# Window attention with the score and value matmuls of two sequences issued together, one ring of seven PSUM banks, and the row maximum subtracted on GpSimd

## What is computed

```python
x = x + 0.5 * ffn_ref(layernorm(x), ...)      # "stack" 0: 6 layers
x = x + attn_ref(layernorm(x), ...)           # a gated state-space scan, 16 states
x = x + 0.5 * ffn_ref(layernorm(x), ...)      # "stack" 1: the same 6 layers again
# one layer of ffn_ref (16 heads of 64, windows of 32):
q, k, v = split(shift_tokens(x) @ Wqkv)
q, k = rotary(l2norm(q) * qs), rotary(l2norm(k) * ks)
sim = where(mask, -max, einsum('bhwie,bhwje->bhwij', q, k_of_this_and_last_window) * 8)
x = softmax(sim) @ v_of_this_and_last_window @ Wo + x
a, gate = split(layernorm(shift_tokens(x)) @ W1 + b1)
x = (a * gelu(gate)) @ W2 + b2 + x
```

## Time and profile before

| | |
|---|---|
| median of 3 runs | 3716.87 us (3713.0 to 3719.67) |
| profiled execution, its own time | 3724.61 us |
| span of its instructions | 3722.6 us |
| stack 0, scan, stack 1, by the slices | about 1690, 350 and 1690 us |

### The profile page before, as it was taken

How to read it: one execution, slowest core, us unless ns; L and a number is a source line. 1 busy time by engine, 2 the same in 40 slices (tenths; PEclk the granted TensorE clock), 3 DMA queues, 4 the chain that set the end, 5 groups by cost and what they waited for, 6 DMA issues and landing times.

```text
span 3722.6 us, 144192 instructions
## 1 busy us (share of the span) xinstructions
PE 3402.5 (91%) x62248; PEld 1871.9 (50%) x62248; DVE 3223.6 (87%) x5344; ACT 2227.8 (60%) x3808; POOL 2052.1 (55%) x1787
## 2 busy tenths in 40 slices
PE   6899999999999999985676799999999999999996
PEld 2455555555555555542333355555555555555553
DVE  5899999999999999874776799999999999999984
ACT  3566576665666666652453466666766667666663
POOL 3666566555666656642433565665656656565552
PEclk8999999999999999996877999999999999999998
DMA  4232332232332322200001332232232332332320
GB/s 126 68 79 70 75 81 73 72 81 70 80 77 70 85 70 72 73 17 12 0 0 54 78 76 73 70 87 69 73 85 67 78 83 67 77 82 66 77 49 24
DMA packets 200483, 250.08 MB, mean 67 GB/s; under 512 B 52012, under 2 KB 95656, under 8 KB 199848
## 3 DMA queue, kind: packets, MB, share of 16 engines
q1 hardware_dynamic: 199848, 240.86, 25.9%
HBM read 36.18 MB, written 3.15 MB: 11 GB/s over the span
## 4 chain that ended last, share of the span: by engine, by line
PE 30%; DVE 12%; issue 4%; ACT 3%; POOL 1%; DMA 1%; SPq 0%; POOLq 0%; DVEq 0%; ACTq 0%
PE general L566 4%; PE attp L580 4%; PE general L628 3%; PE scores L598 3%; PE sums L608 2%; PE general L636 2%; PE general L645 2%; PE general L638 1%; PE proj_k L554 1%; DVE k_ring L1232 1%; DVE sines L752 1%; DVE q_ring L758 1%; DVE probs_t L845 1%; PE proj_q L554 1%; PE proj_q L556 1%
## 5 line engine op out<-in xcount | busy, mean ns | idle before, releaser
L1107 POOL TENSOR_TENSOR k_ring<-k_ring,partner 128x512 f32<-128x512 f32 x384 | 499.0, 1299 | 362.1 <-DMA partner<-sines 359.9
L1116 POOL TENSOR_TENSOR probs<-probs,q_scale 128x512 f32<-128x512 f32 x384 | 401.8, 1046 | 396.8 <-DVE probs L828 396.8
L1122 POOL TENSOR_TENSOR probs<-probs,row_sum 128x512 f32<-128x512 f32 x384 | 407.8, 1062 | 358.3 <-DVE row_sum L839 358.2
L1107 POOL TENSOR_TENSOR q_ring<-q_ring,partner 128x512 f32<-128x512 f32 x384 | 491.2, 1279 | 50.4 <-DMA partner<-sines 50.4
L954 ACT ACTIVATE squares<-proj_q 128x512 f32<-128x512 f32 x384 | 229.0, 596 | 402.4 <-PE proj_q L556 401.0
L580 PEld LDWEIGHTS attp<-probs_t,v_buf 32*64 32x64 f32 x24576 | 393.0, 133 | 147.4 <-issue 141.8
L566 PE MATMUL general<-att,wo 128*128 128x512 f32 x768 | 376.2, 624 | 74.0 <-ACT att L1013 74.0
L580 PE MATMUL attp<-probs_t,v_buf 32*64 32x64 f32 (+1 forms) x24576 | 435.5, 218 | 5.1 <-ACT att L1013 5.1
L752 DVE SCALAR_TENSOR_TENSOR sines<-proj_q,vec,consts 128x512 f32<-128x512 f32 x384 | 278.7, 726 | 170.1 <-ACT squares L954 149.7
L628 PE MATMUL general<-wv,xs 128*32 128x256 f32 x6144 | 413.2, 387 | 3.1 <-DVE rstd L727 1.7
L598 PE MATMUL scores<-k_ring,q_ring 64*32 64x64 f32 (+1 forms) x24576 | 405.0, 215 | 0.0
(11 more groups left out here) (149 smaller groups left out, 6835.5 us busy)
## 6 DMA issues: line engine op xcount, KB each, us to landing
partner<-sines SPq DMA_DIRECT2D x3072, 64.0 KB
wqk_raw<-in_wqkv SPq DMA_DIRECT2D x80, 128.0 KB
wv<-in_wqkv SPq DMA_DIRECT2D x12, 512.0 KB, 4.4
wo<-in_wo SPq DMA_DIRECT2D x12, 512.0 KB, 4.7
w<-in_w SPq DMA_DIRECT2D x12, 341.0 KB, 3.3
base_dram<-x SPq DMA_DIRECT2D x8, 256.0 KB, 2.7
att<-in_wqkv SPq DMA_DIRECT2D x4, 512.0 KB, 5.8
q_ring<-base_dram SPq DMA_DIRECT2D x8, 256.0 KB, 3.1
```

The lines of the kernel that those rows point to most:

```text
L1107: e.tensor_tensor(y, y, partner[:, which, :], ALU.add).then_inc(S[f"rotated_{side}"], 1)
L1116: e.tensor_tensor(y, y, spread_keys(scale), ALU.mult).then_inc(S["q_norms_off"], 1)
L1122: e.tensor_tensor(y, y, spread_keys(row_sum[:, b, :]), ALU.mult).then_inc(S["probs_done"], 1)
```

## The change

- `pe_scores` and `pe_values` take a group of four heads of **both** sequences at once, every second step. For each window they issue the four matmuls of sequence 0 and the four of sequence 1, and for sequence 1 the heads are swapped in pairs (`h = q ^ seq`), so that the eight matmuls name eight different tiles of the array (scores: 64 by 32; values: 32 by 64). Scores go to one bank per sequence, values to four.
- All banks but `sums` form one ring of seven. Each use takes the next bank and waits for the release of the use seven before.
- The row maximum is subtracted on GpSimd (`pool_sub`), one step after the scores; exp, sum and the later stages move one step back. The softmax works on 1024 columns per operation, with two buffers `probs` instead of three. Scores are still two operations.
- The copy of the key norms goes from VectorE to ScalarE (`act_k_inv`); the spread is four matmuls of 256 columns.
- The three gate matmuls and the three gelus stand in one step (p = 1), the value matmuls and products in the next two.
- The order inside a step changes on every engine; `q_scale8` is written by eight activations instead of four; the raw weight loads have three semaphores instead of one; a constant is twice as wide.

```diff
-EXP_LAG = SCORES_LAG + 1
-TURN_LAG = SCORES_LAG + 2
-VALUES_LAG = SCORES_LAG + 3
+OFF_LAG = SCORES_LAG + 1
+EXP_LAG = SCORES_LAG + 2
+TURN_LAG = SCORES_LAG + 3
+VALUES_LAG = SCORES_LAG + 4
-PROBS = 3
+PROBS = 2
...
-        self.hidden = next(((self.item(t, 25 + j), j) for j in range(len(HIDDEN_CUTS)) if self.item(t, 25 + j) is not None), None)
+        self.gates = self.item(t, 25)
+        self.values_of = next(((self.item(t, at), js) for at, js in ((26, (0,)), (27, (1, 2))) if self.item(t, at) is not None), None)
...
     def use(self, key, sem, value):
-        self.of[key] = len(self.uses)
-        self.uses.append((sem, value))
+        at = self.next
+        self.next = (at + 1) % self.banks
+        self.of[key], self.before[key] = at, self.last.get(at)
+        self.last[at] = (sem, value)
...
+            g = [pe_bank(w, ("att", k, n, group, j)) for j in range(4)]
+            for kb in range(NWIN):
                 width = 2 * WIN if kb < NWIN - 1 else WIN
+                for seq in range(CHUNK_SEQS):
+                    for q in range(4):
+                        h = q ^ seq
+                        lhs = v_buf[32 * q:32 * q + 32, n % 2, seq * NWIN + kb, group * DH:(group + 1) * DH]
+                        at = seq * COLS + kb * 64 + WIN
+                        rhs = probs_t[32 * q:32 * q + 32, i % 2, at:at + width]
+                        o = g[2 * seq + h // 2][DH * (h % 2):DH * (h % 2) + DH, kb * WIN:kb * WIN + width]
+                        done = e.matmul(o, lhs, rhs, start=(kb == 0), stop=True, skip_group_check=True)
+            done.then_inc(S["valued"], 1)
...
+            g = [pe_bank(w, ("scores", k, n, group, seq)) for seq in range(CHUNK_SEQS)]
+            for seq in range(CHUNK_SEQS):
+                e.matmul(g[seq][:, :], ident_bf[:, :], mask_bf[:, :], start=True, stop=False, skip_group_check=True)
             for win in range(NWIN):
+                for seq in range(CHUNK_SEQS):
+                    for q in range(4):
+                        h = q ^ seq
+                        slot, r0 = slot_of(n, 2 * group + h // 2), DH * (h % 2)
+                        t0, back = seq * SEQ + win * WIN, WIN if win else 0
+                        qw = qk_ring[0][r0:r0 + DH, slot, t0:t0 + WIN]
+                        kw = qk_ring[1][r0:r0 + DH, slot, t0 - back:t0 + WIN]
+                        o = g[seq][32 * q:32 * q + 32, win * 2 * WIN + WIN - back:(win + 1) * 2 * WIN]
+                        done = e.matmul(o, qw, kw, start=False, stop=True, skip_group_check=True)
             done.then_inc(S["scored"], 1)
...
+        def pool_sub(e, w, k, n, group):
+            i = (k * ITEMS + n) * GROUPS + group
             y = cube(probs[:, i % PROBS, :])
+            w.wait_ge(S["row_max"], i + 1)
+            e.tensor_tensor(y, y, spread_keys(row_max[:, i % 2, :]), ALU.subtract).then_inc(S["max_off"], 1)
```

457 lines of the change are left out of this document (238 added, 219 removed).

## The result

The changed kernel takes 4099.61 us in the median of four runs (4074.35 to 4117.48), beside 3718.27 (3713.0 to 3720.07) for the kernel before on the same chip: 1.102 of it, 95% interval 1.096 to 1.109. The forecast was 3319. The direction is wrong and the miss is 780 us. The profiled run took 4074.35 us, 4072.6 of it span.

What follows compares the result with a forecast made beforehand. TensorE and VectorE were taken to bound the kernel together, the larger counting in each step. Maxima of 58.6 times 0.98, plus 0.8 for the norms, gave a 58.2 us cycle against 66.5, 398 us less over 48 items: 3319 us, range 3180 to 3500.

Steps and rivals of the forecast that it cites:

- the sum that explained 66.5: Item cycle before: per-step maxima of TensorE and VectorE add up to 67.9 us; the measured 66.5 is 0.98 of that.
- The rule: Costing of the changed cycle: larger of TensorE and VectorE per step, summed to 58.6, times 0.98, giving 57.4 us.
- Eight tiles: Score and value bursts: full overlap on eight tiles, 1.0 and 1.1 us for both sequences, saving 8.2 us per item.
- Issue has room: TensorE's score bursts: issue takes 7 ns per matmul, so eight need 54 of the 57 ns and tiles stay the bound.
- Rival 2: Score and value bursts: eight tiles don't overlap or only in part, even steps stay 2.0 us longer, 3630 us; chance 0.10.
- Less switching: TensorE goes to tiled work and back twice, not four times, per pair of steps, saving 1.6 us per item.
- The norms' wait: VectorE's norms, late in p = 0 and needed back first in p = 1: 0 to 1.6 us per item, taken as 0.8.
- The ring, costed at nothing: Seven-bank ring: 13 uses per pair of steps let TensorE run about half a pair ahead, as before; cost nothing.
- The slower rival: GpSimd's 1024-column operations slowed by contention beside VectorE; at 4.0 us each, cycle 72.6 us and time 4010; chance 0.04.
- the five cases: Whole kernel: forecast 0.70, GpSimd pacing odd steps 0.10, tiles not overlapping 0.10, TensorE alone 0.06, slower than before 0.04.

Runs made afterwards that it cites:

- e10: Kernel before, with only the subtraction of the row maximum moved from VectorE to GpSimd: 3686.41 us, 0.991 of before.
- e5: Changed kernel with the score and value loops turned round, one sequence after the other on four tiles at a time: 4038.57 us, 1.086 of before.
- e13: Kernel before, with values directly behind scores and issued three times over, 512 short instructions in a row: 5050.79 us, 1.357 of before.
- e6: Changed kernel with the value matmuls moved to the head of the step on TensorE, ahead of the projections: 4207.42 us, 1.133 of before.
- e2: Changed kernel with the subtraction, merged over both sequences, back on VectorE: 4188.89 us, 1.126 of before.
- e12: Kernel before, with the subtraction on GpSimd and the k_inv copy on ScalarE: 3699.69 us, 0.994 of before.
- e1: Changed kernel with one of the four transfers of each partner-row move, for timing only: 3898.23 us, 1.048 of before.
- e15: Changed kernel with values first and two steps later, last output projection behind the projections, one of four partner-row transfers per move: 3854.1 us, 1.034 of before.
- e3: Changed kernel with the last part of the output projection behind the q and k projections of its step: 4022.12 us, 1.082 of before.
- e16: Kernel before, with the k projection directly behind the q projection on TensorE, other engines' orders unchanged: 3862.86 us, 1.038 of before.
- e4: Changed kernel with the norm operations on VectorE moved ahead of the scores of their step: 4109.11 us, 1.105 of before.
- e11: Changed kernel with values ahead of the projections and, with what follows them, two steps later: 4009.15 us, 1.077 of before.
- e9: Kernel before, with only the value matmuls placed directly behind the score matmuls on TensorE: 3746.68 us, 1.007 of before.

## Why the prediction was wrong, point by point

In short: the gain of the eight tiles was put at 8.2 us an item and is 2.6 of busy time, and the new order, the longer bursts and the ring were put at nothing, where TensorE's waits grew by 459 us.

**What bounds the kernel, and the sum that explained 66.5.** The parts were right, and their use was not. The rule took the larger of TensorE and VectorE in each step and held for the order that had been measured. e10 shows how little VectorE's part weighed: taking 6.1 us an item from it by the forecast's price, a tenth of its work, brought 0.9% (38 us, 0.8 an item). By the rule of the forecast it should have given nearly three times that: with 0.76 less for VectorE in every step the maxima add up to 65.7 instead of 67.9, 2.2 an item. A rule that fits one number with one factor (0.98) had not been tested.

**Eight tiles: the step that failed first.** "Issue has room", 7 ns per matmul, was read from 27 ns at the start of a burst and used for a whole burst. That four tiles were the bound of the old bursts was right (e5). That with eight the tiles would stay the bound was not: TensorE keeps up such a pace for some 24 matmuls, and the last 30 of a score burst start 10.4 ns apart. Eight tiles bring 128 score matmuls to 1.43 to 1.53 us, 11 to 12 ns each, between the two ends of the forecast, 1.0 and 1.96. The middle of an old burst could not have told it, as it shows the pace of the four tiles, 14 ns; no row of before has the pace of issue over 128, so both ends belonged into the range. The term was 2.0 us per group (8.2 an item); the same kernel with four tiles at a time (e5) puts it at 124 us / 192 groups = 0.65 us of busy time (2.6 an item), and in time it is nothing or below, as e5 is the faster one by 61 us. The Trainium skill's rule that I set aside ("TensorE: Matmul & The Clock Gate", section "Wait — 56ns, not 53.3ns?", about 25 ns between starts) is not borne out in its figure, as the 11 to 12 ns measured are under half of it; but its warning, that small matmuls have a floor of their own, was right. Rival 2 (no overlap, 3630) had a part of the truth on the bursts, and not the direction.

**The stops: in no step.** Doubling a burst and setting the second behind it made a run of 512 short instructions where the longest had been 128. It costs 261 us directly. e13 shows that the length of the run alone can do it. No row of before could have priced it; that the change doubled the longest run was visible in the diff, and belonged among the unknown costs with a bound of its own. Parting the bursts (e6) removes three quarters of the stops; a wait of 545 us comes in their place, since an order that brings the values forward has to bring the probabilities forward too.

**Less switching, VectorE, GpSimd, ScalarE.** The work moved as reckoned: VectorE lost 370 us of busy time, 7.7 an item with 8.5 forecast, GpSimd gained 284, 5.9 an item with 8.4 forecast, ScalarE lost 201, 4.2 an item with 4 to 6 forecast, and table loads fell from 506 to 284, 5.9 an item with about five forecast. The 1.6 us an item for less switching has no run of its own. The gain did not reach the time, as neither VectorE nor GpSimd was the bound. Undone alone in the changed kernel the subtraction costs 2.2% (e2), done alone in the one before it wins 0.9% (e10). The copy of `k_inv`, counted as 2.4 us off VectorE, is a small loss (e12).

**The order inside the step, costed at nothing.** The section on the change lists the new order, and the prediction priced only the norms in it. Three of its parts have prices. The rotations of q and k stand side by side, and VectorE waits 349 us for moves for which it waited 31 before: each is four issues and a landing, and each sine buffer is single. Three quarters of the transfers away gives back 200 us (e1) or 154 (e15). The output projection now follows its own inputs within the step, 204 us of waits on VectorE and 78 us of time (e3). And TensorE's two projections together are worth 3.8% in the kernel before (e16); how much of that is in the changed kernel, where VectorE's order follows, no run separates. SyncE's queue was not among the queues that I followed.

**The norms' wait.** Taken as 0.8 us an item, bounds 0 to 1.6; the row shows 174.8 us in 48 waits, 3.6 an item. Most of it is ScalarE, which comes late from v and then needs 3.3 us. Moving the norms on VectorE does nothing to the time (e4); in the order of e15 it is 23.7 us, and VectorE's split of the tokens waits 221 us for ScalarE instead.

**The ring, costed at nothing.** "13 uses per pair of steps over seven banks let TensorE run about half a pair ahead". The rows say otherwise: the values wait for the bank of a q projection (52.2 us, 67 times), a layer norm for that of a k projection (32.7 us), and in e11 the values for a gelu's bank (83.6 us). The cover was counted in banks and not by who holds them longest. The kernel before had banks of their own for projections, scores and values. What the ring costs in time no run tells.

**How the 748 us between forecast and profile split.** Forecast for the profiled execution: 398 us less, made of 456 less work of TensorE and 58 more waits. Measured: 350 more, made of 109 less work (3406 to 3298, span less waits) and 459 more waits. So 347 us are work that wasn't saved and 401 are waits. Of the 347, about 180 are the longer bursts (0.93 us per group, 1.53 + 1.5 against 2.1, 192 groups). The half clock, with its bound of 204, can be the rest; no run separates it from the switching that was forecast to be saved. Of the waits 263 are stops or other time without a releaser.

**The slower rival.** Its chance was 0.04 and it named GpSimd's contention, with 3.5 us per operation as the point from which it decides. Measured are 1.92 us, so the time is slower by other mechanisms than its own. The range missed because none of the five cases had a term for the stops or for the order inside the step.

**What stays open.** After the values are moved, the output projection is later and three quarters of the moves are gone (e15), 133 us remain over the kernel before, with TensorE waiting 660 us instead of 316. The ring, ScalarE's order (VectorE waits 420 us for the squares there) and two buffers `probs` instead of three are the candidates; no run kept the order and gave the old banks back, and none has the third buffer.

## What to carry to other kernels

Don't take an issue rate from a burst's first nanoseconds; where its middle is held by something else, no row has that rate, and the range must hold both ends. Ask of every merge how many short instructions it puts in a row. In this kernel TensorE was 91% busy and the order around it fitted what waits for what; a new order has to be priced queue by queue, transfers and bank holders included, even when it moves no work. Make the separable part first: the subtraction alone was worth 0.9%, and the whole change lost 10%.

## What the runs showed of the hardware that was not expected

- TensorE, matmuls of 64 columns with a weight load each: 13.2 and 14.5 ns from start to start on four tiles (scores and values of the kernel before, the mean over bursts of 64), about 10.6 to 11.1 on eight (bursts of 128 without a stop), and 5 to 7 for the first 24 score matmuls of such a burst.
- Such instructions stop arriving in runs of 512: 154 stops of 1.7 us on average in the changed kernel, 328 of 1.5 us in e13, two in runs of 256 on four tiles (e9), 37 and 58 in runs of 256 on eight (e6, e11), none in the kernel before. Every stop of the changed kernel and of e13 ends 1.16 to 1.68 us behind the end of a 16 KB packet of the instruction queue.
- TensorE's granted clock stood at 1.2 GHz in the window behind the one in which TensorE was busy for 2.97 of 5 us, and at 0.90 of full in the next. A stop of 1.5 us in nearly every step left the mean at 0.967 (e13); 909 us of waits left it at 0.888 (e6).
- One DMA of partner rows holds SyncE's queue for 0.70 us when issued back to back (5.58 for eight).
- GpSimd takes 1.92 us for 1024 columns where two of 512 take 2.09.
